# A layer's change in a vision transformer kernel: DMA order, weight loads, the class rows' layout and the position projections

## What is computed

```python
L, H, D, DH, DF = (4, 16, 256, 64, 1024)
for i in range(L):
    qkv = h @ W_qkv[i]
    q, k, val = jnp.split(qkv, 3, axis=-1)
    kr = (r @ W_r[i]).reshape(s_len, H, DH)
    AC = jnp.einsum('bqhd,bkhd->bhqk', q + u, k)
    BD = jnp.einsum('bqhd,khd->bhqk', q + v, kr)
    prob = jax.nn.softmax((AC + BD) * inv_sqrt_d, axis=-1)
    vec = jnp.einsum('bhqk,bkhd->bqhd', prob, val).reshape(b, s_len, H * DH)
    h = layer_norm(h + vec @ W_o[i], ln1_g[i], ln1_b[i])
    ff = jax.nn.relu(h @ W_ff1[i] + b_ff1[i]) @ W_ff2[i] + b_ff2[i]
    h = layer_norm(ff, ln2_g[i], ln2_b[i])
```

## Time and profile before

| what | value |
|---|---|
| median of 3 executions | 2784.75 us |
| the profiled execution's own time | 2779.74 us |
| its span in the profile | 2777.6 us |
| PE busy | 2232.7 us, 80% |
| DVE busy | 1803.0 us, 65% |
| ACT busy | 1618.7 us, 58% |
| POOL busy | 1189.3 us, 43% |
| mean granted clock of PE, share of full | 0.953 |

### The profile page before, as it was taken

The page is one execution under the profiler, slowest core; times in us unless marked ns, Lnnn a source line. Parts: engine busy times, 40 slices in busy tenths (PEclk is TensorE's granted clock), DMA queues, the critical chain, the costliest instruction groups (busy, mean ns, idle before and its releaser), DMA issues. The chain is left out here.

```text
span 2777.6 us, 61222 instructions
## 1 busy us (share of the span) xinstructions
PE 2232.7 (80%) x19212; PEld 1644.3 (59%) x19213; DVE 1803.0 (65%) x5446; ACT 1618.7 (58%) x5077; POOL 1189.3 (43%) x2202
## 2 busy tenths in 40 slices
PE   0168988988789988988888889888889989833995
PEld 0146666666566666666566666665666666522663
DVE  8746777776567777766667777766677777633333
ACT  2146767766557767765666666666666666611221
POOL 3045555554355555544455555544554454202002
PEclk9589999999999999999999999999999999965998
DMA  5353333434543333354433333344333333155002
GB/s 166 91 143 90 97 92 95 98 95 140 161 112 93 93 92 93 92 153 108 135 99 95 95 94 92 94 144 146 97 95 97 95 98 95 40 146 175 28 28 76
DMA packets 387569, 289.49 MB, mean 104 GB/s; under 512 B 45256, under 2 KB 360768, under 8 KB 385856
## 3 DMA queue, kind: packets, MB, share of 16 engines
q1 hardware_dynamic: 380800, 268.87, 36.8%
q10 hardware_dynamic: 4864, 12.68, 1.3%
q0 software_dynamic: 1600, 4.23, 0.5%
HBM read 125.54 MB, written 59.09 MB: 66 GB/s over the span
## 5 line engine op out<-in xcount | busy, mean ns | idle before, releaser
L1197 ACT ACTIVATE E<-E,nb 128x257 f32<-128x257 f32 x1024 | 514.3, 511 | 83.6 <-DVE nb L1363 83.6
L1363 DVE CUSTOM_DVE_ANT_0 E<-bk,cb 128x257 f32<-128x257 f32 x1024 | 390.6, 418 | 107.9 <-PE bk L1012 107.5
L917 PE MATMUL bk<-hin,w_sb 128*128 128x257 f16 x3072 | 428.8, 277 | 17.1 <-ACT rel L1131 9.3
L1325 DVE TENSOR_TENSOR pt<-bk,pt 128x512 f16<-128x512 f32 x512 | 354.1, 692 | 70.1 <-ACT pt L1184 61.9
L965 PE MATMUL bk<-ident,E 128*128 128x128 f32 x2048 | 323.8, 281 | 87.6 <-ACT E L1197 61.0
L917 PEld LDWEIGHTS bk<-hin,w_sb 128*128 128x128 f16 x3072 | 298.5, 99 | 75.7 <-ACT rel L1131 14.5
L813 POOL TENSOR_SCALAR rq<-rel 128x257 f16<-128x257 f32 x256 | 104.6, 409 | 525.5 <-ACT rel L1131 525.2
L965 PEld LDWEIGHTS bk<-ident,E 128*128 128x128 f32 x2048 | 221.8, 141 | 169.4 <-ACT E L1197 152.5
L1184 ACT ACTIVATE pt<-bk 128x512 f16<-128x512 f32 x512 | 307.7, 601 | 10.3 <-PE bk L965 10.0
L1011 PE MATMUL bk<-kh,qs 128*128 128x257 f16 x1024 | 258.5, 278 | 47.7 <-DMA hin<-hd_dram 47.5
L1012 PE MATMUL bk<-kl,qs 128*128 128x257 f16 x1024 | 258.5, 278 | 0.0
(11 more groups left out here) (270 smaller groups left out, 4386.3 us busy)
## 6 DMA issues: line engine op xcount, KB each, us to landing
qs<-rq SPq DMA_DIRECT2D x256, 128.5 KB, 3.5
kh<-rk SPq DMA_DIRECT2D x256, 128.5 KB, 3.3
kl<-rk SPq DMA_DIRECT2D x256, 128.5 KB, 3.6
wf<-in_w_dram SPq DMA_DIRECT2D x168, 128.0 KB, 2.4
w_split_dram<-wh SPq DMA_DIRECT2D x168, 128.0 KB, 2.1
wf<-in_we_dram SPq DMA_DIRECT2D x96, 128.0 KB, 2.2
we_split_dram<-wh SPq DMA_DIRECT2D x96, 128.0 KB, 1.7
w_sb<-w_split_dram SPq DMA_DIRECT2D x12, 1024.0 KB, 7.0
```

The costliest lines, as they stand in the source:

```text
L917: r = mm(bank[4 + s % 2][:, 0:S], wcol(a, C_QKV, k, 3 * HD, chunk_at(s)), hin[:, m, k, :], start=i == 0, stop=i == 5)
L1197: act.activation(E[:, h % 2, qt, :], E[:, h % 2, qt, :], ACT.Exp, bias=nb[:, 2 * h + qt:2 * h + qt + 1], scale=-1.0, accum_out=sums[:, qt, ...
L1325: v.tensor_tensor(pt[:, h, 1, :, 0:IMG], bank[2 + h % 2][:, :].rearrange("p (k s) -> p k s", k=QT), pt[:, h, 0, :, 0:IMG], ALU.subtract).t ...
L1363: v.tensor_tensor_reduce(E[:, h % 2, qt, :], bank[qt][:, 0:S], cb[:, h, :], -SCORE, 3e38, ALU.add, ALU.min, nb[:, 2 * h + qt:2 * h + qt + ...
```

## The change

- `hin` and `vbd` of the next body are issued at the end of this one, ahead of the last three chunk stores; `hres` follows those stores. PE waits for `hin` at the first slot, not at head 0.
- Chunks are split in another order, W_r first (`ORDER`), so that W_r and the q and k columns of the next layer can be loaded during image 6 (g = 6, 14, 22), in three DMAs; the v columns come as two DMAs at the start of image 7, and W_o, W_1 and W_2 at the start of the ENTRY body.
- In a CLOSING body the 8 position projections and the 16 slots are spread over all 16 heads, by turns two and one a head. DVE takes over ACT's eight copies. `position_term` moves from behind the v projection to head 8, its copy to head 9, its stores to head 11, and the load of `cb` to the end of the head loop.
- `vbd_dram` holds three copies of 16 short rows per image in place of 128 rows. The class rows are stored by 3 DMAs, not 12, and `vbd` is loaded by four DMAs of 12 rows, not one of 128. The zeroing at the start writes 51 rows per image.

```diff
-VBD_IMAGE = P * HD
+VBD_COPY = H * HD + H * DH
+VBD_IMAGE = 3 * VBD_COPY
+def vbd_rows(vbd, b, j):
+    return vbd[b, :].rearrange("(c n) -> c n", c=3)[:, 4 * j * HD:4 * (j + 1) * HD].rearrange("c (i n) -> c i n", i=4)
+def vbd_diagonal(vbd, copy):
+    first = copy * VBD_COPY
+    return vbd[:, first:first + H * (HD + DH)].rearrange("b (h n) -> b h n", h=H)[:, :, 0:DH]
...
+ORDER = tuple(range(C_R // SPLIT, C_1 // SPLIT)) + tuple(range(C_R // SPLIT)) + tuple(range(C_1 // SPLIT, PLAIN))
...
-        slots = lambda h, kind: () if not kind.next else (h,) if not kind.closing else () if h < NP else (2 * h - H, 2 * h - H + 1)
+        def slots(h, kind):
+            if not kind.next:
+                return ()
+            if not kind.closing:
+                return (h,)
+            return tuple(i - NP for i in range((3 * h + 1) // 2, (3 * h + 4) // 2) if i >= NP)
+        def position_slots(h, kind):
+            return tuple(i for i in range((3 * h + 1) // 2, (3 * h + 4) // 2) if i < NP) if kind.closing else ()
...
-                sp.dma_start(vbd_rows(io["vbd"], b), vbd[:, :]).then_inc(zero_out, 16)
+                sp.dma_start(io["vbd"][b, :].rearrange("(p n) -> p n", p=3 * (H + 1)), vbd[0:3 * (H + 1), :]).then_inc(zero_out, 16)
...
                 for copy, t in enumerate((0, 0, 1)):
-                    for j in range(4):
...
-                hold(vbd_out, atl(192, 192))
+                    sp.dma_start(vbd_diagonal(io["vbd"], copy), vcl[:, t, :].rearrange("b (h d) -> b h d", h=H)).then_inc(vbd_out, 16)
+                hold(vbd_out, atl(48, 48))
...
+            def load_vbd(g):
+                hold(o_done, 8 * g)
+                for j in range(4):
+                    sp.dma_start(vbd[32 * j:32 * j + 12, :], vbd_rows(io["vbd"], g % B, j)).then_inc(vbd_in, 16)
+            def load_hin(g):
+                hold(v_done, 4 * g + 4)
+                sp.dma_start(flat(hin), io["hd"][(g + 1) % B]).then_inc(hin_in, 16)
+            def load_hres(g):
+                hold(ff1_done, 8 * g)
+                sp.dma_start(flat(hres), io["hd"][g % B]).then_inc(hres_in, 16)
...
+                if kind is CLOSING:
+                    for k in range(KC):
+                        c = C_QKV + k * 3 * HD + 2 * HD
+                        load_w("w_v_in", c, c + HD, l + 1)
+                for c in range(2 if plan else 0):
+                    load_chunk(c)
+                if kind.entry:
+                    load_w("w_o_in", C_O, C_2, l)
+                    load_w("w_1_in", C_1, C_O, l)
+                    hold(ff2_done, at(2, 0))
+                    load_w("w_2_in", C_2, W_COLS, l)
+                if kind is MIDDLE and b == B - 2:
...
                     load_w("w_r_in", C_R, C_1, l + 1)
-                    load_w("w_qkv_in", C_QKV, C_R, l + 1)
...
+                if kind is MIDDLE and b == B - 2:
+                    for k in range(KC):
+                        c = C_QKV + k * 3 * HD
+                        load_w("w_qk_in", c, c + 2 * HD, l + 1)
+                late = max(len(plan) - 3, 0)
+                for c in range(late):
+                    store_chunk(c)
+                if kind.next:
+                    if not after.entry:
+                        load_vbd(at.g + 1)
+                    if after.next:
+                        load_hin(at.g + 1)
+                for c in range(late, len(plan)):
+                    store_chunk(c)
+                if kind.next:
+                    load_hres(at.g + 1)
...
-                        r = mm(bank[2][32 * j:32 * j + 32, 0:S], wm[:, 2 * j + of, :], kr16[:, 2 * j + of, :], start=of == 0, stop=of == 1)
+                        r = mm(bank[7][32 * j:32 * j + 32, 0:S], wm[:, 2 * j + of, :], kr16[:, 2 * j + of, :], start=of == 0, stop=of == 1)
...
-                if kind.next:
-                    pe.wait_ge(hin_in, at(16, 32))
...
+                    if 0 in slots(h, kind):
+                        pe.wait_ge(hin_in, at(16, 32))
+                        if kind.closing:
+                            pe.wait_ge(kr_ok, atl(8, 8))
+                            pe.wait_ge(w_sem["w_qk_in"], atl1(32, 0))
...
+                    if h == NP and kind.closing:
+                        pe.wait_ge(vy_ok, at(1, 0))
+                        position_term(atl)
...
                 if kind.closing:
+                    pe.wait_ge(w_sem["w_v_in"], atl1(32, 0))
...
+            def take_kr(atl, j):
+                v.wait_ge(kr_done, atl(8, j + 1))
+                v.tensor_copy(kr16[:, j, :], bank[4 + j % 2][:, 0:S]).then_inc(kr_ok, 1)
```

More of the change, by code:

```diff
@@ L519, in iterations, with kind_of @@
 def iterations(eng, body):
-    for l in range(L):
-        for b in range(B):
-            if b == 0:
-                kind = ENTRY if l else OPENING
-            elif l == L - 1:
-                kind = FINAL if b == B - 1 else TAIL
-            else:
-                kind = CLOSING if b == B - 1 else MIDDLE
-            body(At(eng, l * B + b), l, b, kind)
+    for g in range(L * B):
+        body(At(eng, g), g // B, g % B, kind_of(g))
 PLAIN, CENTRED = C_O // SPLIT, (W_COLS - C_O) // SPLIT
 E_CHUNKS = E_COLS // SPLIT
+ORDER = tuple(range(C_R // SPLIT, C_1 // SPLIT)) + tuple(range(C_R // SPLIT)) + tuple(range(C_1 // SPLIT, PLAIN))
+def kind_of(g):
+    l, b = divmod(g, B)
+    if b == 0:
+        return ENTRY if l else OPENING
+    if l == L - 1:
+        return FINAL if b == B - 1 else TAIL
+    return CLOSING if b == B - 1 else MIDDLE
 def chunk_plan(b, kind):
@@ L761, in body @@
                     store_vcls(At(sp, l))
-                    sp.dma_start(vbd[:, :], vbd_rows(io["vbd"], b)).then_inc(vbd_in, 16)
+                    load_vbd(at.g)
                 if kind.next:
                     stack(at1, 1)
-                for c in range(len(plan)):
-                    hold(split_lo, n0 * 2 + (c + 1))
-                    sp.dma_start(plan[c][1], wh[:, c % 2, :, :]).then_inc(split_out[c % 2], 16)
-                    if c + 2 < len(plan):
-                        load_chunk(c + 2)
-                if kind.closing:
+                if kind is MIDDLE and b == B - 2:
[14 more added lines that the diff above has]
+                    load_hres(at.g + 1)
+                if kind is CLOSING or (kind is MIDDLE and b == B - 2):
                     for i in range(2):
-                        hold(split_out[i], (n0 + 4) * 16)
-                    hold(wo_done, at(2, 2))
-                    load_w("w_o_in", C_O, C_2, l + 1)
+                        hold(split_out[i], (n0 + len(plan) // 2) * 16)
             def store(at, b):
@@ L1214, in body @@
                         class_v(atl)
+                    if h == NP + 3 and kind.closing:
+                        spread_position_term(atl)
                     act.wait_ge(e_ok, at(32, 2 * h + 2))
@@ L1377, in body @@
                         class_v(atl)
+                    if h == NP + 1 and kind.closing:
+                        position_term(atl)
                     if h == H - 3:
```

71 lines of the change are left out of this document (23 added, 48 removed).

## The result

The changed kernel takes 2743.31 us (median of 4 executions, 2739.50 to 2745.91); the kernel before takes 2784.39 beside it. The ratio is 0.9857, with a 95% interval of 0.9841 to 0.9872. That is 41 us less, where 70 were forecast: the direction was right, but the time lies 5 us above the upper end of the range.

The account below looks back on a forecast made before the run. It took 99.2 us of excess in long bodies around layer changes and after the opening as reachable: 26.3 stay, 72.9 saved less 2.5 in the opening, 70.4 off 2779.7 gives 2709.3, plus 5.0 for the median: 2714 us. Range 2698 to 2738.

Parts of the forecast that it names:

- a new wait in CLOSING: CLOSING's feed-forward: PE waits for DVE, held by the last chunk's mean; 1.1 us a body, from 0 to some 8.
- if PE waits for DVE's mean in CLOSING: One of the signs listed in advance that would show the forecast wrong, in CLOSING bodies; no size of its own.
- The CLOSING loop: CLOSING's head loop, projections and slots spread over 16 heads: last head at 31.5 us, bounds 29.9 and 34.3; 3.2 us stay.
- the 0.2: Behind CLOSING's head loop: the last head has one slot, not two, so 0.2 us of excess stays.
- The opening: Start of the kernel: fewer class stores gain 3 us, 51-row zero stores may lose up to 8; 2.5 us lost taken.
- Rival 1: Opening and ENTRY: 51-row stores use 3 DMA engines, class stores 12.4 us later, stack 8.3; 2724 us, chance 0.20.
- the waits for `hin`: PE's 47.5 us of waits in 8 places: all but the opening one go, and the slow clock with them.
- The copies: CLOSING loop: eight copies of some 0.4 us, moved from ACT to DVE, hide in idle time; otherwise 3.3 us per loop.
- The three stores in place of twelve: ENTRY's class stores: fewer stores free SP by 3.1 us, more than PE's 2.86 us wait for vbd; 0.3 us left.
- Ordinary bodies: Bodies away from layer changes and the opening: unchanged at 67.7 us.
- The second: CLOSING: loop at its upper bound and DVE held 5 us by the last chunk; 20 us more, 2734, chance 0.12.

Follow-up runs that it names:

- the first experiment: Changed kernel with DVE's two late chunk means of a CLOSING body moved behind its feed-forward's hidden rows: 2721.92 us, ratio 0.978.
- The POOL experiment: Late means moved, 128-row zero stores, hin early in opening (2715.35 us), plus POOL's layer-norm gain one head earlier and low half after the last CLOSING slot: 2709.71 us.
- the ninth experiment: Against the version with late means moved, 128-row zero stores and hin early in the opening (2715.35 us): all chunk stores ahead of vbd and hin again: 2759.81 us.
- the third experiment: Changed kernel with one more chunk store, and so the last chunk's load, ahead of vbd and hin in CLOSING bodies alone: 2742.27 us, ratio 0.9859.
- the tenth: Against the version with late means moved, 128-row zero stores and hin early in the opening (2715.35 us): eight position-projection copies back on ACT: 2717.36 us.

## Why the prediction was wrong, step by step

**The step that failed: "a new wait in CLOSING".** The prediction named the instruction (DVE's mean of a late chunk, ahead of its hidden rows), named what could make it large (the load of `cb` at the loop's end, "up to some 8 if the load of `cb` ... delays the chunks before it"), and then took 1.1 us, near the lower end, with no row to say so. It was 22 us in three bodies, and the first experiment gave back 21. Its own sign of being wrong, "if PE waits for DVE's mean in CLOSING", is what came. The row that spoke for the upper end was there: the last chunk's load went out at 728.31, 4.3 us ahead of DVE's mean at 732.63, and the second half of `stack` and all the chunk stores ahead of it would now stand behind the start of a 2056 KB load. In that trace the load had landed 1.9 us before the mean (1.0 and 2.3 in the other two CLOSING bodies), and any delay beyond this slack was bound to be passed on in full. The mechanism was right, its reason only in part: of the two reasons given, the place behind `hin` was nothing beside an early `cb` and at most some 0.8 us a body without it, the load of `cb` more than half. What is left of the 2 us of DVE's wait in a body comes from the gain itself: DVE arrives 6 us earlier, its chunks 3. The forecast had counted the shorter loop and the shorter tail as gains and not asked what they overtake.

**The CLOSING loop** was taken at 31.5 us, with bounds of 29.9 and 34.3. It was 33.4, 33.4 and 33.7: inside the bounds, and 1.9 to 2.2 more than forecast. The argument that POOL "is as full as PE" was made, and then ACT's relief was given weight in its place. The POOL experiment shows 1.5 us of this to be its layer norm between the slots. With the means moved, the body is 72.4 and not 74 us, because the stretch behind the loop came out shorter than forecast: neither the 0.2 nor the 1.1 us is left there.

**The opening** was taken at 2.5 us lost, "the middle" of a gain of 3 and a loss of 8. It lost 7.2 (256.9 against 249.7 at the start of image 1). Rival 1 had it right: few engines for 51 rows, a DMA share of 0.18 to 0.20. Its figures were 12.4 us for the class stores, where 9.4 were measured (163.07 against 153.65), and 8.3 for `stack`, measured 5.7. Its other half, `vbd` slower by 1.4 us in each ENTRY, did not come: PE's waits there fell from 2.86 us to 1.51, and to 1.04 and 1.18 at the other changes. Between bounds far apart the middle is no estimate.

**Right:** the waits for `hin` are gone, and the clock of ENTRY rose from 0.92 to 0.98. ENTRY takes 73.3, 71.5 and 73.0 us where 71.3 were forecast; the two longer ones have 3.4 us at half clock each, some 40 us into the body, and the one of 71.5 has none. The bodies behind it take 67.6 to 68.5, where 68.2 were. The reason given for the waits, that SP issues `hin` behind W_o, held by the stores' landing, covers at most the three ENTRY bodies, 18.8 of the 47.5 us. The four bodies with no W_o ahead of `hin`, 17.0 us, had it behind the last stores alone; the ninth experiment, with `hin` behind all stores, costs 44.5 us in bodies that are by now shorter, and leaves W_o's own part open. The copies cost next to nothing on either engine. The three stores in place of twelve gave SP 3 us, and the four loads of `vbd` in place of one took most of it back (3.01 us of issues against 0.34), which the prediction left out.

**Ordinary bodies** were forecast unchanged; the 20 took 4.9 us more. Most of it is the clock. Four of them (against one before) have a stretch of 3.4 us at half clock, some 37 us into the body, and take 69.4 us on average; the other 16 take 67.97, where the 19 before took 67.92. The number of such stretches differs between versions that leave these bodies alone: the third experiment has none and its 20 bodies take 1359.9 us, the tenth has six and takes 1366.9. So the forecast holds for the bodies' own work. Why the clock falls there in some executions stays open.

**The rivals.** The second (CLOSING gives its gain back, 2734, chance 0.12) is the one that came, larger than priced: 23.3 us beyond the forecast of CLOSING in place of 20, and the first (2724, 0.20) came with half its price beside it, 4.7 us in the opening and none in ENTRY. The range ended at 2738, 4 us above the dearest of the three: it holds no sum of two. Two that don't exclude each other, 20 and some 5 us above 2714, already reach 2739, outside it. CLOSING missed by 3.3 us more than its rival said, which makes 2742. The table's other terms are 8.3 us in sum, and all but about 1 of them goes against the 7 us by which its two profiles stand differently to their medians.

## What to carry to other kernels

When a large load is moved earlier, list what the other queues must issue while it runs, and find the engine that waits in order for the last of them: a few microseconds on the queue become a stop of everything behind one small operation. Put operations that wait for a DMA behind the ones that feed the critical engine. A load whose consumer is early belongs ahead of stores that nobody awaits, and more so the closer those stores come to the end of the body.

## What the runs showed of the hardware

- A store of 102 KB as 51 rows takes far longer than as 128: eight of them land within 20.7 us against 6.6, at a DMA share of 0.18 to 0.20 against 0.68, and one takes 0.94 us to issue on average against 0.47 (7.54/8, 3.75/8).
- A DMA of 12 rows of three copies takes 0.76 us to issue (3.05/4), where one of 128 rows took 0.34. Splitting a load can cost the queue more than the bytes save.
- Behind the issue of the 2056 KB load of `cb`, on ACT's queue, three pairs of SP's issues took 2.67 to 3.78 us where most take 1.3 to 1.9, and half a `stack` of 12 DMAs 13.4 us in place of 9.5.
- In an idle stretch of 7.9 us on PE (729.6 to 737.55) the granted clock fell to 0.50, that is 1.2 GHz in place of 2.4, at 734.0, and was back at 740.8; the feed-forward's matmuls of 737.55 to 740.8 ran at it.
